# A two-layer graph network with skip LSTMs: the second convolution's positive part moves from ScalarE to VectorE, and the next round's normalisations start two cells later

## The chip, the cores and the metric

The kernel runs on one core of a Trainium2 chip. The metric is the device time of one execution in microseconds. PE is TensorE (the matrix engine), DVE is VectorE, ACT is ScalarE, POOL is GpSimd, SP is the engine that issues the DMAs.

## What is computed

Two blocks, each with a layer norm in front and a residual sum behind. `x` is 128 graphs of 128 nodes with 128 features. The first block works in the eigenbasis of a Laplacian; the change doesn't touch it. The second is the one of interest:

```python
h = jnp.maximum(_layernorm(x, axis=-1), 0.0)
# inside _L1_gnn_ref(h, adj, ...)
h = jax.nn.relu(jnp.einsum('ts,bsh->bth', adj, x @ Wg0 + bg0))
h = jax.nn.relu(jnp.einsum('ts,bsh->bth', adj, h @ Wg1 + bg1))      # the second relu is the one that moves
for p in range(1, MAX_SKIP + 1):                                    # 1 to 4
    nw = Tv // p
    wins = h[:, :nw * p, :].reshape(Bv * nw, p, Hd)
    last = _lstm_last(Wih[p - 1], Whh[p - 1], bih[p - 1], bhh[p - 1], wins)
    idx = jnp.arange(nw) * p + (p - 1)
    h = h.at[:, idx, :].set(last.reshape(Bv, nw, Hd))
```

So for every skip p from 1 to 4 an LSTM of p steps runs over all windows of p nodes, and its last hidden state replaces the window's last node.

## The kernel before

**Stages.** The first 440 us or so compute the eigenvectors (small steps on DVE, ACT, PE and POOL), with parts of the first block behind them until about 748 us. From there to the end the second block runs, on PE, DVE and ACT, with one table load of ACT ahead of it and none inside.

**Rounds and streams.** The second block has 8 rounds (`ROUNDS`). A round holds 4 streams i = 0 to 3 of 4 graphs each. Streams 0 and 1 are one pair (A), 2 and 3 the other (B). Each stream owns two PSUM banks.

**The order.** The list `ORDER` (L155) is the same for PE, ACT and DVE, and each of them walks it in its own program (`second_layer`, L562, L822, L1471), with semaphores between them. An entry (n, i) is step n for stream i. Steps are LIN, ZED (x times the second weight), CONV (times the adjacency), then 11 cells, then TURN. Pair B runs one step behind pair A: after LIN for all four the order is ZED 0, ZED 1, CONV 0, CONV 1, ZED 2, ZED 3, cell0 0, cell0 1, CONV 2, CONV 3, cell1 0, cell1 1, cell0 2, cell0 3, cell2 0 and so on. The cells are `CELLS` (L41): cell0 and cell1 are the two halves of p = 1, cell2 and cell3 the steps j = 0, 1 of p = 2, cell4 to cell6 those of p = 3, cell7 to cell10 those of p = 4. A cell has 256, 256, 168 or 128 columns for p = 1 to 4. Cells with j = 0 have 3 gates and need only the input product; the others have 4 gates and twice the products. The text calls the cell c of stream i "cell c/i".

**One cell.** PE computes the gates (L805, L810 and L815, L818). ACT takes I, G and F out of PSUM with sigmoid or tanh (L552), DVE forms the new state c (L1429 for j = 0; L1432, L1433, L1435 otherwise), ACT takes tanh(c) (`cell_tanh`, L560), DVE multiplies it with the output gate (`hidden`, L1444, L1446). The next cell of the stream on PE waits for that: with j = 0 for all of it, otherwise the input products wait for the tanh and the recurrent products for `hidden`. Both ACT and DVE are one entry late with the second half: `cell_tanh` and `hidden` of a cell are issued inside the next entry of `ORDER`, behind that entry's own first work (`waiting`). ACT issues the output gate behind that.

**The two places that change.** At CONV, ACT waits for `conv_ready[i]` and writes the positive part of 128x512 PSUM elements into `HS[i]` (L574). It reads 512 elements in sequence and writes them with a step of 4 elements, as `HS` holds the four graphs of a node side by side. `H_ready[i]` then lets cell0 of the stream start on PE. `normalize` (L525) forms one graph's normalised input of the next round, 128x128 elements; there are 4 for each stream, issued on ACT behind the output gate of the cells listed in `NORM_AT` (L157), which are 3, 5, 6 and 8. The fourth increments `h1_ready[i]`, for which `mix` (L754) waits at the end of the round on PE. The last round has no normalisations.

**Around them.** DVE at LIN, ZED and TURN handles 128x512 elements each out of PSUM (L1477, L1481, L1455), and copies the next round's `mix` (L1451). In round 0 alone DVE also takes statistics for later normalisations behind some cells (`last_statistics`, L1458: four instructions L1397 behind each stream's cell 3, 5 and 6). SP stores each stream's result (L297) after TURN.

Of the kernel before, what the change touches and what calls it, by code (L numbers as in the profile page):

```python
# [6 lines left out]
ALU = mybir.AluOpType  # L7
ACT = mybir.ActivationFunctionType
# [18 lines left out]
GB = 4  # L27
# [13 lines left out]
CELLS = [(1, 0, 0, N // 2), (1, 0, N // 2, N // 2)] + [(p, j, 0, N // p) for p in range(2, SKIPS + 1) for j in range(p)]  # L41
# [18 lines left out]
def build(nc, t_in, out):  # L60
    with ExitStack() as ctx:
# [3 lines left out]
        def sem(name):  # L65
            return ctx.enter_context(nc.semaphore(name))
# [72 lines left out]
        def per_stream(name):  # L139
# [7 lines left out]
        y_ready, z_ready, z_kept, conv_ready, H_ready = map(per_stream, ("y", "z", "zk", "conv", "H"))  # L147
# [5 lines left out]
        MIX, LIN, ZED, CONV, CELL = range(5)  # L153
        TURN = CELL + len(CELLS)
        ORDER = [(LIN, i) for i in range(STREAMS)]             + [(n, i) for slot in range(ZED, TURN + 1) for pair, n in (((0, 1), slot), ((2, 3), slot - 1))  # L155
               for i in pair if n > LIN] + [(TURN + 1, i) for i in range(STREAMS)] + [(TURN, i) for i in (2, 3)]
        NORM_AT = [c for c, (_, j, _, _) in enumerate(CELLS) if j][:GB]  # L157
        adj_in = sem("adj_in")
        consts = sem("consts")
        v_ = sem("v_")  # L160
# [65 lines left out]
        gI, gF, gG, gO, cS, HS, tS, hS = ([pieces[STREAMS * c + i] for i in range(STREAMS)] for c in range(8))  # L226
# [25 lines left out]
        def batches(v):  # L252
            return v.rearrange("p (b t) -> p b t", b=GB)

        def nodes(v):
            return v.rearrange("p (n b) -> p n b", b=GB)
# [5 lines left out]
        bank = [[banks[2 * i + c % 2][:] for c in range(4)] for i in range(STREAMS)]  # L262
# [160 lines left out]
        def _(act):  # L423
# [98 lines left out]
            def normalize(it, i, b, done):  # L522

                at = bass.ds(batch(it, i, b), 1)
                ins = nc.scalar.activation(hs[i][:, b * D:(b + 1) * D], X[:, at, :].rearrange("p b d -> p (b d)"),  # L525
                                           ACT.Relu, bias=ln[:, 3, at], scale=ln[:, 2, at])
                if b == GB - 1:
                    ins.then_inc(done[i], 1)
# [15 lines left out]
            def gates(it, c, i, qs):  # L544

                p, j, _, nw = CELLS[c]
                T = GB * nw
                for q in qs:
                    if q == GATE_F and j == 0:
                        continue  # L550
                    at = (p - 1) * 4 + q
                    last = nc.scalar.activation(gate_out[q][i][:, 0:T], gate(i, q, T),  # L552
                                                ACT.Tanh if q == GATE_G else ACT.Sigmoid, bias=bias[:, at:at + 1])
                if q == GATE_F:
                    last.then_inc(acts_ready[i], 1)

            def cell_tanh(it, c, i):
                T = GB * CELLS[c][3]
                act.wait_ge(cell_ready[i], it * len(CELLS) + c + 1)
                nc.scalar.activation(tS[i][:, 0:T], cS[i][:, 0:T], ACT.Tanh).then_inc(tanh_ready[i], 1)  # L560

            def second_layer(it, more):  # L562
                act.wait_ge(tables, it + 1)

                nc.scalar.activation(act_scratch[:], ln[:, 2, 0:1], ACT.Sigmoid).then_inc(tables, 1)
                waiting = None
                for n, i in ORDER:
                    c = n - CELL
                    if n == LIN:
                        act.wait_ge(lin_kept[i], it + 1)  # L570
                        nc.scalar.activation(yS[i], linS[i], ACT.Relu).then_inc(y_ready[i], 1)
                    elif n == CONV:
                        act.wait_ge(conv_ready[i], it + 1)
                        nc.scalar.activation(nodes(HS[i]).rearrange("p n b -> p b n"), batches(bank[i][0]),  # L574
                                             ACT.Relu).then_inc(H_ready[i], 1)
                    elif CELL <= n < TURN:
                        act.wait_ge(gates_ready[i], it * len(CELLS) + c + 1)
                        gates(it, c, i, (GATE_I, GATE_G, GATE_F))
                    if waiting:
                        cell_tanh(it, *waiting)  # L580
                        waiting = None
                    if CELL <= n < TURN:
                        gates(it, c, i, (GATE_O,))
                        waiting = (c, i)
                        if more and c in NORM_AT:
                            normalize(it + 1, i, NORM_AT.index(c), h1_ready)

            half = ROUNDS // 2 - 1
            with nc.scalar.Fori(0, half) as it:
                second_layer(it, True)  # L590
            act.wait_ge(ln_done, 3)
            with nc.scalar.Fori(half, ROUNDS - 1) as it:
                second_layer(it, True)
            second_layer(ROUNDS - 1, False)

        B = [b[:, 0:N] for b in banks]
# [248 lines left out]
        def _(dve):  # L845
            t = Tally(v_)
            V = nc.vector
# [308 lines left out]
            for f in range(2, F):  # L1156
                c = f % 2
# [266 lines left out]
            def cell(it, c, i):  # L1424
                p, j, _, nw = CELLS[c]
                T = GB * nw
                dve.wait_ge(acts_ready[i], it * len(CELLS) + c + 1)
                if j == 0:
                    V.tensor_tensor(cS[i][:, 0:T], gI[i][:, 0:T], gG[i][:, 0:T], ALU.mult).then_inc(cell_ready[i], 1)  # L1429
                    return  # L1430
                parts = it * PARTS + sum(2 for _, jj, _, _ in CELLS[:c] if jj)
                V.tensor_tensor(gI[i][:, 0:T], gI[i][:, 0:T], gG[i][:, 0:T], ALU.mult).then_inc(cell_part[i], 1)  # L1432
                V.tensor_tensor(gF[i][:, 0:T], gF[i][:, 0:T], cS[i][:, 0:T], ALU.mult).then_inc(cell_part[i], 1)  # L1433
                dve.wait_ge(cell_part[i], parts + 2)
                V.tensor_tensor(cS[i][:, 0:T], gI[i][:, 0:T], gF[i][:, 0:T], ALU.add).then_inc(cell_ready[i], 1)  # L1435

            def hidden(it, c, i):
                p, j, w0, nw = CELLS[c]
                T = GB * nw

                dve.wait_ge(tanh_ready[i], it * len(CELLS) + c + 1)

                if j < p - 1:
                    V.tensor_tensor(hS[i][:, 0:T], gO[i][:, 0:T], tS[i][:, 0:T], ALU.mult).then_inc(hidden_ready[i], 1)  # L1444
                else:
                    V.tensor_tensor(window(HS[i], p, j, w0, nw), nodes(gO[i][:, 0:T]), nodes(tS[i][:, 0:T]),  # L1446
                                    ALU.mult).then_inc(hidden_ready[i], 1)

            def keep_mix(it, i):
                dve.wait_ge(mix_ready[i], it + 1)  # L1450
                V.tensor_copy(mixS[i], bank[i][0]).then_inc(mix_kept[i], 1)  # L1451

            def residual(it, i):
                dve.wait_ge(turned_ready[i], it + 1)
                V.tensor_tensor(X[:, group(it, i), :], X[:, group(it, i), :], batches(bank[i][1]),  # L1455
                                ALU.add).then_inc(sum_ready[i], 1)
# [14 lines left out]
            def second_layer(it, more, extra=None):  # L1471

                waiting = None
                for n, i in ORDER:
                    if n == LIN:
                        dve.wait_ge(lin_ready[i], it + 1)
                        V.tensor_tensor(batches(linS[i]), batches(bank[i][2]),  # L1477
                                        G0[:].unsqueeze(1).to_broadcast([N, GB, N]), ALU.add).then_inc(lin_kept[i], 1)
                    elif n == ZED:
                        dve.wait_ge(z_ready[i], it + 1)  # L1480
                        V.tensor_tensor(batches(zS[i]), batches(bank[i][3]),  # L1481
                                        bg1B[:].unsqueeze(1).to_broadcast([N, GB, D]), ALU.add).then_inc(z_kept[i], 1)
                    elif CELL <= n < TURN:
                        cell(it, n - CELL, i)
                    elif n == TURN:
                        residual(it, i)
                    elif n > TURN and more:
                        keep_mix(it + 1, i)
                    if waiting:
                        hidden(it, *waiting)  # L1490
                        waiting = None
                    if CELL <= n < TURN:
                        waiting = (n - CELL, i)
                    if extra:
                        extra(n, i)

            for i in range(STREAMS):
                keep_mix(0, i)
            second_layer(0, True, last_statistics)
            with V.Fori(1, ROUNDS - 1) as it:  # L1500
                second_layer(it, True)
# [24 lines left out]
```

## Time and profile before

| | us |
|---|---|
| median of 3 runs | 1515.49 |
| their range | 1513.96 to 1518.14 |
| the profiled execution, own time | 1516.81 |
| its span in the trace | 1515.1 |
| rounds 1 to 6 of the second block, from 848 to 1418 us, each | 94.9 |
| PE, busy share of the span | 79% |
| DVE, ACT, busy share of the span | 73%, 62% |

Times in the rows are microseconds from the start of the span, unless they are marked ns. A line of a timeline gives start, duration, engine and line, what is written and read, and how many like it were merged; in square brackets the idle time of the engine before it, and what ended that. PEld is PE's load of weights. All durations come from one profiled execution. A fp32 matmul shows as two passes, so a product in the program is two rows' worth in the trace.

### The profile page before, as it was taken

How to read it: one execution, taken by the hardware profiler on the slowest of the kernel's cores; microseconds unless marked ns; L12 is line 12 of the kernel's file. 1: busy time of each engine (PE TensorE's matmuls, PEld its weight loads, DVE VectorE, ACT ScalarE, POOL GpSimd, SP SyncE). 2: the span in 40 equal slices, each digit the busy share in tenths (PEclk: the TensorE clock that was granted, in tenths of full speed). 3: DMA queues.
4: the chain of work that ended last, by engine and by line, in shares of the span. 5: the costliest groups of instructions: out<-in, count | busy, mean ns of one | idle time of the engine just before them, and what ended most of it. 6: DMA issues, size and time to landing. Idle time of an engine off the chain costs nothing.

```text
span 1515.1 us, 26850 instructions
## 1 busy us (share of the span) xinstructions
PE 1196.2 (79%) x7121; PEld 1069.9 (71%) x7121; DVE 1107.1 (73%) x5944; ACT 943.2 (62%) x3339; POOL 508.6 (34%) x1426
## 2 busy tenths in 40 slices
PE   5777777777536400179999999999999999999998
PEld 4566666666435300168789899898998989989897
DVE  8999999999999999958747656455564554645545
ACT  4666666666349600012478687786877868778676
POOL 0288888888888888830000200000000000000000
PEclk9999999999869855579999999999999999999999
DMA  9300000000000000003100000000000000000001
GB/s 269 79 1 1 1 1 1 1 1 1 1 1 1 1 0 0 1 28 105 36 1 2 28 0 28 0 0 28 0 28 0 0 28 0 26 2 0 28 1 29
DMA packets 43630, 28.80 MB, mean 19 GB/s; under 512 B 1520, under 2 KB 39440, under 8 KB 43536
## 3 DMA queue, kind: packets, MB, share of 16 engines
q1 hardware_dynamic: 43536, 27.81, 6.7%
q14 instruction: 67, 0.55, 0.1%
q8 instruction: 27, 0.44, 0.1%
HBM read 19.42 MB, written 8.39 MB: 18 GB/s over the span
## 4 chain that ended last, share of the span: by engine, by line
PE 52%; POOL 33%; issue 7%; DVE 6%; ACT 2%; POOLq 0%; ACTq 0%; DVEq 0%
PE bank L815 13%; PE bank L805 10%; POOL leaf L388 9%; PE bank L810 8%; PE bank L818 7%; POOL leaf L386 6%; POOL leaf L403 3%; PE bank L735 2%; PE bank L787 2%; PE bank L779 2%; PE bank L743 2%; PE bank L773 2%; PE bank L750 2%; PE bank L758 2%; ACT BIG L552 1%
## 5 line engine op out<-in xcount | busy, mean ns | idle before, releaser
L815 PE MATMUL bank<-spare,wT 128*128 128x256 f32 (+2 forms) x1408 | 311.3, 321 | 0.0
L552 ACT ACTIVATE PV<-bank,bias 128x256 f32<-128x256 f32 (+2 forms) x704 | 304.0, 435 | 0.0
L552 ACT ACTIVATE BIG<-bank,bias 128x128 f32<-128x128 f32 (+2 forms) x544 | 227.6, 418 | 121.0 <-PE bank L818 101.9
L815 PEld LDWEIGHTS bank<-spare,wT 128*128 128x128 f32 x1408 | 234.8, 191 | 13.2
L805 PE MATMUL bank<-spare,wT 128*128 128x128 f32 (+2 forms) x1088 | 228.1, 320 | 4.1 <-DVE spare L1446 2.7
L1432 DVE TENSOR_TENSOR BIG<-BIG,PV 128x128 f32<-128x128 f32 (+2 forms) x192 | 63.0, 328 | 205.9 <-ACT BIG L552 205.9
L805 PEld LDWEIGHTS bank<-spare,wT 128*128 128x128 f32 x1088 | 168.7, 190 | 22.5 <-DVE spare L1446 9.1
L818 PE MATMUL bank<-spare,wT 128*128 128x128 f32 (+2 forms) x768 | 169.7, 303 | 0.0
L810 PE MATMUL bank<-spare,wT 128*128 128x128 f32 (+2 forms) x768 | 141.6, 307 | 3.8 <-DVE spare L1444 1.4
L618 PE MATMUL bank<-ident 128*128 128x2 f32 x254 | 74.3, 362 | 88.6 <-DVE ident L963 87.5
L388 POOL TENSOR_TENSOR leaf<-leaf 128x1 f32<-128x1 f32 x240 | 136.7, 570 | 20.0
L560 ACT ACTIVATE spare<-spare 128x256 f32<-128x256 f32 (+2 forms) x352 | 134.4, 382 | 6.9 <-DVE spare L1435 6.9
L618 PEld LDWEIGHTS bank<-ident 128*128 128x128 f32 x254 | 63.6, 311 | 99.6 <-DVE ident L963 98.2
L1429 DVE TENSOR_TENSOR spare<-BIG,PV 128x256 f32<-128x256 f32 (+2 forms) x160 | 60.8, 380 | 95.7 <-ACT PV L552 95.6
L818 PEld LDWEIGHTS bank<-spare,wT 128*128 128x128 f32 x768 | 125.2, 191 | 3.3
L810 PEld LDWEIGHTS bank<-spare,wT 128*128 128x128 f32 x768 | 113.8, 191 | 14.2 <-DVE spare L1444 10.9
L386 POOL TENSOR_SCALAR leaf<-leaf 128x1 f32<-128x1 f32 x240 | 93.3, 389 | 23.4
L610 PE MATMUL bank<-ones,sc 128*128 128x1 f32 x2 | 0.6, 348 | 120.5 <-DVE sc L1269 120.5
L442 ACT ACTIVATE sc<-bank 128x1 f32<-128x1 f32 x127 | 21.7, 171 | 116.1 <-PE bank L618 116.0
L623 PE MATMUL bank<-A,UC 128*128 128x127 f32 (+63 forms) x254 | 87.5, 442 | 7.3 <-DVE UC L926 0.8
L1209 DVE SCALAR_TENSOR_TENSOR PV<-RC,m,PV 128x4 f32<-128x4 f32 x508 | 90.6, 220 | 0.0
L610 PEld LDWEIGHTS bank<-ones,sc 128*128 128x128 f32 x2 | 0.5, 313 | 120.6 <-issue 120.6
(405 smaller groups left out, 3000.8 us busy)
## 6 DMA issues: line engine op xcount, KB each, us to landing
spare<-in_x SPq DMA_DIRECT2D x32, 256.0 KB, 3.8
out<-X SPq DMA_DIRECT2D x32, 256.0 KB, 2.4
spare<-in_L_gnn_Wih SPq DMA_DIRECT2D x4, 256.0 KB, 5.2
spare<-in_L_gnn_Whh SPq DMA_DIRECT2D x4, 256.0 KB, 4.6
W<-in_L_gnn_W SPq DMA_DIRECT2D x2, 64.0 KB, 2.7
Wg<-in_L_gnn_Wg SPq DMA_DIRECT2D x2, 64.0 KB, 2.4
adj<-in_adj SPq DMA_DIRECT2D x1, 64.0 KB, 2.0
X<-in_x SPq DMA_DIRECT2D x4, 0.5 KB, 17.0
```

The costliest lines, as they stand in the source:

```text
L386: op(TS(am[:, i + 1:i + 2], rho[:, i:i + 1], ne16[:, i:i + 1], am[:, i + 1:i + 2], ALU.mult, ALU.add))
L388: op(TT(rho[:, i + 1:i + 2], am[:, i + 1:i + 2], neg16[:, 0:1], ALU.pow))
L552: last = nc.scalar.activation(gate_out[q][i][:, 0:T], gate(i, q, T), ACT.Tanh if q == GATE_G else ACT.Sigmoid, bias=bias[:, at:at + 1])
L560: nc.scalar.activation(tS[i][:, 0:T], cS[i][:, 0:T], ACT.Tanh).then_inc(tanh_ready[i], 1)
L618: nc.tensor.matmul(banks[7][:, 0:2], x_wide, ident[:, t:N + 1:N - t], start=True, stop=True).then_inc(s_ready, 1)
L623: nc.tensor.matmul(banks[1][:, live(k)], u_c.to_broadcast([N, N]), A[:, live(k)], start=True, stop=True).then_inc(pb_ready, 1)
L805: last = nc.tensor.matmul(gate(i, q, T), wT[:, 0, p - 1, q * D:(q + 1) * D], xt, start=True, stop=(j == 0))
L810: last = nc.tensor.matmul(gate(i, q, T), wT[:, 1, p - 1, q * D:(q + 1) * D], hS[i][:, 0:T], start=False, stop=True)
L815: last = nc.tensor.matmul(gate(i, q, T), wT[:, 0, p - 1, q * D:(q + 1) * D], xt, start=True, stop=(j == 0))
L818: last = nc.tensor.matmul(gate(i, q, T), wT[:, 1, p - 1, q * D:(q + 1) * D], hS[i][:, 0:T], start=False, stop=True)
L1209: s.did(V.scalar_tensor_tensor(out=nx, in0=RC[:, last + lane:last + lane + live], scalar=M[2][:, row:row + 1], in1=nx, op0=ALU.mult, op1=A ...
L1432: V.tensor_tensor(gI[i][:, 0:T], gI[i][:, 0:T], gG[i][:, 0:T], ALU.mult).then_inc(cell_part[i], 1)
```

## The change

`NORM_AT` takes the first four cells with j > 0 and p > 2: cells 5, 6, 8 and 9 in place of 3, 5, 6 and 8. The positive part at CONV is issued by DVE as a `tensor_scalar` with a maximum against 0, at the same entry of the order and with the same wait, source, destination and semaphore; ACT has nothing of its own to do at CONV any more.

```diff
-        NORM_AT = [c for c, (_, j, _, _) in enumerate(CELLS) if j][:GB]
+        NORM_AT = [c for c, (p, j, _, _) in enumerate(CELLS) if p > 2 and j][:GB]
@@ ACT, second_layer
-                    elif n == CONV:
-                        act.wait_ge(conv_ready[i], it + 1)
-                        nc.scalar.activation(nodes(HS[i]).rearrange("p n b -> p b n"), batches(bank[i][0]),
-                                             ACT.Relu).then_inc(H_ready[i], 1)
@@ DVE, second_layer
+                    elif n == CONV:
+                        dve.wait_ge(conv_ready[i], it + 1)
+                        V.tensor_scalar(nodes(HS[i]).rearrange("p n b -> p b n"), batches(bank[i][0]), 0.0, None,
+                                        ALU.max).then_inc(H_ready[i], 1)
```

## Rows read from the trace of the kernel before

**Rows 1.** The page: busy time of the engines, and the granted clock in slices.

```profile
PE 1196.2 (79%) x7121; PEld 1069.9 (71%) x7121; DVE 1107.1 (73%) x5944; ACT 943.2 (62%) x3339; POOL 508.6 (34%) x1426
...
PEclk9999999999869855579999999999999999999999
```

**Rows 2.** Windows: busy time of each engine in round 3, then granted clock.

```profile
1038.00:1133.00 95.00, 94.06 (x626) 86.31 (x625) 51.05 (x153) 73.61 (x225) 0.00 (x0) 1.00 0.04 11
```

**Rows 3.** Waits in round 3: who waited for whom, total us, times, longest.

```profile
PEld bank L810 <- DVE spare L1444: 1.4, 4, 0.4
PEld bank L805 <- DVE spare L1446: 1.1, 2, 0.7
PEld bank L805 <- ACT spare L560: 0.5, 2, 0.4
```

**Rows 4.** Timeline of PE: first products of cells 1/0, 1/1, 0/2 and 0/3.

```profile
1051.02 0.70 PE L805 MATMUL bank<-spare,wT 128*128 128x256 f32 x2
...
1052.55 0.70 PE L805 MATMUL bank<-spare,wT 128*128 128x256 f32 x2
...
1053.95 0.59 PE L805 MATMUL bank<-spare,wT 128*128 128x256 f32 x2
...
1055.25 0.59 PE L805 MATMUL bank<-spare,wT 128*128 128x256 f32 x2
```

**Rows 5.** Timeline of ACT and DVE at CONV of pair B, round 3.

```profile
1050.55 0.42 DVE L1446 TENSOR_TENSOR spare<-PV,spare 128x256 f32<-128x256 f32 x1
1050.73 1.10 ACT L574 ACTIVATE spare<-bank 128x512 f32<-128x512 f32 x1
...
1051.59 0.45 ACT L560 ACTIVATE spare<-spare 128x256 f32<-128x256 f32 x1
1051.91 1.10 ACT L574 ACTIVATE spare<-bank 128x512 f32<-128x512 f32 x1
1052.07 0.43 DVE L1446 TENSOR_TENSOR spare<-PV,spare 128x256 f32<-128x256 f32 x1 [1.10 <-ACT spare L560]
```

**Rows 6.** Groups by shape: busy us, mean ns, idle before. Last: L533's instructions, ns.

```profile
L574 ACT ACTIVATE spare<-bank 128x512 f32<-128x512 f32 x4 | 4.2, 1111 | 1.5 <-PE bank L787 1.5
...
L1481 DVE TENSOR_TENSOR spare<-bank,bg1B 128x512 f32<-128x512 f32 x4 | 2.8, 692 | 2.7 <-PE bank L779 2.7
...
L533 ACT ACTIVATE PV<-bank,b x32: 687/687/687, 662.8 to 741.1; 128x512 f32<-128x512 f32 x32
```

**Rows 7.** Timeline of DVE at pair A's CONV and pair B's ZED, round 3.

```profile
1043.02 0.69 DVE L1481 TENSOR_TENSOR spare<-bank,bg1B 128x512 f32<-128x512 f32 x1 [0.20 <-PE bank L779]
1044.06 2.04 ACT L574 ACTIVATE spare<-bank 128x512 f32<-128x512 f32 x2 [1.47 <-PE bank L787]
...
1045.85 0.69 DVE L1481 TENSOR_TENSOR spare<-bank,bg1B 128x512 f32<-128x512 f32 x1 [2.14 <-PE bank L779]
```

**Rows 8.** Timeline at cell 3's normalisation: ACT, DVE, then PE's cells 4.

```profile
1070.58 0.50 ACT L525 ACTIVATE ahead<-X,ln 128x128 f32 x1
...
1070.96 0.48 ACT L552 ACTIVATE BIG<-bank,bias 128x256 f32<-128x256 f32 x1
...
1072.18 0.42 DVE L1446 TENSOR_TENSOR spare<-PV,spare 128x256 f32<-128x256 f32 x1
...
1072.65 0.55 PE L805 MATMUL bank<-spare,wT 128*128 128x168 f32 x2
...
1085.13 0.45 PE L805 MATMUL bank<-spare,wT 128*128 128x168 f32 x2
```

**Rows 9.** Timeline of PE: what follows each of the two cells 4 of Rows 8.

```profile
1073.61 1.08 PE L805 MATMUL bank<-spare,wT 128*128 128x256 f32 x4
...
1085.99 0.45 PE L805 MATMUL bank<-spare,wT 128*128 128x168 f32 x2
```

**Rows 10.** Timeline of ACT at cell 9 of pair B, and the PE row behind it.

```profile
1122.72 0.37 ACT L552 ACTIVATE BIG<-bank,bias 128x128 f32<-128x128 f32 x1 [0.45 <-PE bank L818]
...
1123.85 0.71 PE L805 MATMUL bank<-spare,wT 128*128 128x128 f32 x4 [0.18 <-ACT spare L560]
...
1124.49 0.31 ACT L560 ACTIVATE spare<-spare 128x128 f32<-128x128 f32 x1 [0.43 <-DVE spare L1435]
```

**Rows 11.** Timeline of DVE in round 0, behind cell 3 of stream 0.

```profile
785.39 0.87 DVE L1397 BATCH_NORM_STATS2 stats<-X 128x6 f32<-128x128 f32 x4
```

## The prediction

> **What bounds the kernel.** I read the page first, then the windows of the second block, then the waits of one round, then the timeline at each of PE's waits. The page's busy shares [rows 1] average over stages with different limits: over the span DVE is nearly as busy as PE. The change works only in the second block, so its windows count, and there the picture is plain: in round 3 PE is busy 94.06 of 95.00 us, ACT 73.6, DVE 51.1, and the granted clock is 1.00, the 2.4 GHz level [rows 2]. Rounds 1 to 6 read the same to 0.1 us. PE is the bound of this stage. An engine that is relieved gives nothing by itself; only what shortens a wait of PE does.
>
> The waits of the round name those places: PE's weight loads wait 4 times for `hidden` ahead of the recurrent products (1.4 us), twice for `hidden` ahead of a cell with j = 0 (1.1 us), twice for the tanh (0.5 us) [rows 3], 3.0 us in a round and 24 us in eight. That is about all that could be won by anything that leaves the matmuls alone. For each of the places I followed in the timeline what PE waited for, and asked whether ScalarE's positive part (L574) or the normalisation of cell 3 lies in that chain.
>
> **The positive part leaves ACT.** It is issued 32 times at 1.11 us [rows 6], 4 in a round, so ACT loses 4.4 us of its 73.6. ACT is not the bound; what counts is who is queued behind. For pair A (streams 0, 1) ACT issues it while PE is still at pair B's ZED, and nothing on PE waits. For pair B it stands in front of the tanh of cell 0/1: L574 starts at 1050.73, that tanh only 0.86 us later, at 1051.59; `hidden` of cell 0/1 follows at 1052.07 on DVE, idle for 1.10 us before it, and ends at 1052.50 [rows 5]. PE starts cell 1/1 at 1052.55 [rows 4]. This is one of the two j = 0 waits. Its price is read from the cells' lengths on PE: cell 0/2 takes 1055.25 - 1053.95 = 1.30 us undisturbed; cell 1/0 takes 1.53 and cell 1/1 1.40 [rows 4]. The first waited itself for cell 0/0, and its restart shows 0.10 in its own length, which stays, as no L574 is ahead of that. So 1.53 + 1.40 - 1.30 - 1.30 - 0.10 = 0.23 us is the price of the wait of cell 1/1, its restart included. Without L574 the tanh can start at 1050.73, and ends 0.45 later at 1051.18. PE would be free for cell 1/1 at 1051.02 + 1.40 = 1052.42.
>
> **The positive part joins DVE.** Four instructions in a round, on an engine idle for 44 of 95 us [rows 2]. The trace has no `tensor_scalar` of this form, so its length d is bounded. The nearest row for the source and size is L1481, 128x512 out of PSUM on DVE: 0.69 us [rows 6]. It writes in sequence, though, and the new one writes with a step of 4 elements. ACT shows what that step can cost: L574 takes 1.11, L533 with the same source and size but a plain destination 0.687 [rows 6], so 0.42 us more. Upper end 0.69 + 0.42 = 1.11; lower end 0.69. I take the upper half, about 0.95: if the memory's side sets the pace, DVE's slower base hides part of the 0.42.
>
> The Trainium skill says, in "Advanced Engine Details and Errata", section Memory Cachelines, that successive accesses run at full rate only inside the same 16-byte line of SBUF, and that a new line for each access costs. Here every one of the 512 writes of four bytes lands in a new line. The L574 and L533 rows agree with it [rows 6]; the page gives no price for DVE, and by a step that costs nothing the sum would be the one for d = 0.69.
>
> What is queued behind it on DVE: for pair A, the ZED of pair B. Conv 0 is out at 1044.06, where L574 starts; two positive parts of 0.95 to 1.11 end at about 1046.0 to 1046.2, and L1481 of stream 2, which starts at 1045.85 after an idle of 2.14 [rows 7], is 0.1 to 0.4 us late. PE uses its result only at pair B's CONV, behind two whole cells; hidden. If that cover were gone it would cost that 0.1 to 0.4. For pair B, the positive part of stream 2 stands in front of `hidden` of cell 0/1, exactly as L574 stood in front of the tanh. DVE is free for it at about 1050.55 + 0.35 = 1050.90 (the 0.42 us instructions start 0.35 apart; conv 2 is out by then, as L574 started at 1050.73 without idle). So `hidden` of cell 0/1 ends at 1050.90 + d + 0.42 at the latest: 1052.01 for 0.69, 1052.27 for 0.95, 1052.43 for 1.11. PE wants it at 1052.42. With d = 0.95 the wait is gone, 0.23 us; with 1.11 it begins to return. The next positive part, of stream 3, ends before 1053.4 and its cell 0/3 runs on PE from 1055.25 - 0.23.
>
> **The normalisation of cell 3 goes to cell 9.** Four per stream as before, so ACT's sum is unchanged. At cell 3 of stream 1, L525 starts at 1070.58 and the gates of cell 2/2 at 1070.96: it holds ACT 0.38 us [rows 8]. On these gates hangs the state of cell 2/2, which DVE forms ahead of `hidden` of cell 3/1, at 1072.18 to 1072.60, and PE starts cell 4/1 at 1072.65 [rows 8]. Cell 4/1 takes 0.96 us, an undisturbed cell 4 takes 0.86 [rows 8, 9]: a restart of 0.10 us. PE was ready at about the same instant, so the 0.38 us on ACT buys these 0.10 and no more. The large part of the wait in front, at cell 4/0, comes straight from PE through gates, state and `hidden`, with ACT idle ahead of it; no normalisation is in it. In round 0 the statistics L1397 hold DVE for 0.87 us there [rows 11], and nothing is gained; the last round has no normalisations. So 6 x 0.10.
>
> What it costs at cell 9: behind pair B's output gate ACT was idle 0.45 us until the gates of cell 9/3 came from PE at 1122.72, and 0.43 us before the tanh at 1124.49 [rows 10]. A normalisation holds ACT 0.38, so both fit, by 0.07 and 0.05 us. They must: PE's cell 10/2 waits for the tanh behind those gates already, with 0.18 us idle [rows 10]. If the cover failed, each 0.1 us of overrun would cost 0.7 us in seven rounds. For pair A the idle times are as long and PE has two cells of pair B as cover. `h1_ready` comes one cell later, and PE asks for it only behind all four cells 10. SP's stores and POOL have no part in either move.
>
> **The sum.** 8 x 0.23 + 6 x 0.10 = 2.4 us. Against the profiled execution's own 1516.81 that is 1514.4; this execution lies 1.32 above the median of the runs, so the median becomes 1515.49 - 2.4 = 1513.1, or 0.16% less. About 0.3% (4.5 us) is what a measurement of this kernel can tell from no change, so the forecast is "no difference".
>
> **Rivals.**
> (a) The wait comes back in another coat: if d is 1.2 to 1.35, `hidden` of cell 0/1 ends at about the old 1052.50 or a little behind. The 1.84 us are lost or turned, only the 0.6 stay: 1514.9 to 1516. For it: the step's cost, unseen on DVE. Against: even ACT's extra of 0.42 gives 1.11.
> (b) Slower: the strided write on DVE costs several times as much. It pays from d = 1.35 upwards; at d = 2.0 `hidden` of cell 0/1 ends at 1050.90 + 2.0 + 0.42 = 1053.3, 0.9 us after PE wants it, plus 0.1 restart, in place of 0.23: 0.77 a round, 8 x 0.77 - 0.6 = 5.6 us more, 1521.1. Against it: neither bound reaches there.
> (c) More is gained than the chains show: if the wait at cell 4/0 (longest 0.7 us [rows 3]) shrinks too once ACT is lighter, 8 x 0.55 = 4.4 more, 1508.7. Against it: ACT idles ahead of the gates it stems from.
> (d) Normalisations at cell 9 overrun their slot by 0.1 to 0.2 us in seven rounds, 0.7 to 1.4: 1514.
>
> **How the numbers follow.** Forecast 0.58, (a) 0.15, (b) 0.08, (c) 0.08, (d) 0.11. The range takes the forecast with the ends of d, (a), (d), and the 1 to 2 us by which medians of so few runs differ: 1510.3 to 1516.9. Faster by over 0.3% (under 1510.9) is (c) with a little of the forecast's edge, 0.10; slower (over 1520.0) is (b), 0.07; within, 0.83.
>
> **What would show it.** A DVE row of L574's shape with d between 0.69 and 1.11; cells 1/0 and 1/1 on PE at 1.40 and 1.30 in place of 1.53 and 1.40; cell 4/1 at 0.86; the loops' rounds 0.33 us shorter than 94.9; PE's wait at cell 10/2 unchanged at 0.18. The prediction is wrong if d is above 1.3, if a new wait of PE stands at a cell 1 or at a cell 10, or if a round changes by more than 0.6 us.

## The result and the profile after

| | before | after |
|---|---|---|
| median, 15 runs each | 1516.02 us | 1512.95 us |
| ratio | | 0.9979, 95% interval 0.9971 to 0.9987 |
| profiled execution, own time | 1516.81 us | 1513.86 us |
| rounds 2 to 6 of the second block, each | 94.87 us | 94.45 us |

The change saves 0.21%, 3.1 us of medians. The forecast was 2.4 us, called "no difference", since about 0.3% was taken as the least that a measurement of this kernel can tell. With 15 runs each the interval is clear of 1, so as little as 0.2% can be told; it leaves room for a saving between 2.0 and 4.4 us, and the rounds say more exactly what the change did.

The page after has the engines' shares moved as the edit says: DVE up by 27 us, ACT down by 29, PE down by 3.4 [rows 1].

```profile
PE 1192.8 (79%) x7121; PEld 1069.7 (71%) x7121; DVE 1134.5 (75%) x5976; ACT 913.9 (60%) x3307; POOL 509.2 (34%) x1426
...
PEclk9999999999869855579999999999999999999999
```

The chain that ended last, after, gives the rounds: start in the span, duration, and what it was. The first product of LIN marks each round (L769 after is L773 before; lines behind L571 moved up by 4 on ACT's side).

```profile
942.32 3.44 PE bank L769 x8
...
1036.77 3.44 PE bank L769 x8
...
1131.23 3.44 PE bank L769 x8
...
1225.68 3.44 PE bank L769 x8
```

1131.23 - 1036.77 = 94.46 (94.45 as the mean of rounds 2 to 6); before it was 94.87. In this round of after, the waits of PE's weight loads for other engines (who waited for whom, us in total, times, longest) are:

```profile
PEld bank L806 <- DVE spare L1440: 1.4, 4, 0.4
PEld bank L801 <- DVE spare L1442: 0.7, 1, 0.7
PEld bank L801 <- ACT spare L560: 0.5, 2, 0.4
```

Against [rows 3] one line has changed: ahead of cells with j = 0 there is one wait where there were two. The timeline of PE shows the cells of [rows 4] and [rows 8, 9] after:

```profile
1050.04 0.70 PE L801 MATMUL bank<-spare,wT 128*128 128x256 f32 x2
1051.44 0.59 PE L801 MATMUL bank<-spare,wT 128*128 128x256 f32 x2
1052.73 0.59 PE L801 MATMUL bank<-spare,wT 128*128 128x256 f32 x2
...
1071.41 0.45 PE L801 MATMUL bank<-spare,wT 128*128 128x168 f32 x2
1072.27 1.03 PE L801 MATMUL bank<-spare,wT 128*128 128x256 f32 x4
```

Cell 1/0 now takes 1051.44 - 1050.04 = 1.40 us and cell 1/1 1.29, against 1.53 and 1.40: 0.24 us. Cell 4/1 takes 0.86 against 0.96, and the first four rows of cell 3/2 behind it 1.03 against 1.08. Both kernels issue the same matmuls in the same order, so the start of each row can be compared, counted from the start of the round; the text calls that "product for product". In round 3 the two kernels differ in five steps only: 0.132 and 0.104 us at cell 1/1, 0.023 and 0.104 at cell 4/1, 0.054 at cell 3/2. That is 0.417 of the 0.42.

What took the positive part's place, on ACT and DVE after (as [rows 5] before):

```profile
1049.57 0.42 DVE L1442 TENSOR_TENSOR spare<-PV,spare 128x256 f32<-128x256 f32 x1
1049.74 0.42 ACT L560 ACTIVATE spare<-spare 128x256 f32<-128x256 f32 x1
1049.90 1.07 DVE L1481 TENSOR_SCALAR spare<-bank 128x512 f32<-128x512 f32 x1
...
1050.81 0.41 DVE L1442 TENSOR_TENSOR spare<-PV,spare 128x256 f32<-128x256 f32 x1
```

The tanh of cell 0/1 follows its neighbour at once, the positive part takes 1.07 us on DVE, and `hidden` behind it starts 0.91 us after it, not 1.07. It ends at 1051.22, and PE starts cell 1/1 at 1051.44 without a wait.

In round 0 only the first of the two gains shows, 0.23 us at cell 1/1, and in the last one too (93.34 against 93.62 from its first product to PE's end), as forecast. Round 1 is not like rounds 2 to 6, though the prediction read rounds 1 to 6 as the same: from LIN to LIN it took 95.20 us before and 94.57 after. Of these 0.63 us 0.20 lie at the start of ZED; round 0, from LIN to LIN, became only 0.04 shorter, so rounds 0 and 1 together gain 0.67, which is 0.24 + 0.42 within 0.01.

### The profile page after: what moved, and what is told of

Its sections match the earlier page's. It is cut to its first block, busy times and chain, and to the rows that moved or that the text cites. A ratio compares the mean times of both kernels' runs of the same rounds, so it can differ in the third digit from the quotient of the medians.

```text
span 1512.1 us, 26850 instructions
## 1 busy us (share of the span) xinstructions
PE 1192.8 (79%) x7121; PEld 1069.7 (71%) x7121; DVE 1134.5 (75%) x5976; ACT 913.9 (60%) x3307; POOL 509.2 (34%) x1426
## 4 chain that ended last, share of the span: by engine, by line
PE 52%; POOL 34%; issue 7%; DVE 6%; ACT 2%; POOLq 0%; ACTq 0%; DVEq 0%
PE bank L811 13%; PE bank L801 9%; POOL leaf L388 9%; PE bank L806 8%; PE bank L814 7%; POOL leaf L386 6%; POOL leaf L403 3%; PE bank L731 2%; PE bank L783 2%; PE bank L739 2%; PE bank L775 2%; PE bank L769 2%; PE bank L746 2%; PE bank L754 2%; ACT BIG L552 1%
## 5 line engine op out<-in xcount | busy, mean ns | idle before, releaser
L560 ACT ACTIVATE spare<-spare 128x256 f32<-128x256 f32 (+2 forms) x352 | 133.1, 378 | 4.2 <-DVE spare L1431 3.9
```

## The experiments

Rounds are read as above, from the starts of LIN in rounds 2 to 6. They repeat within 0.02 us in a trace (0.04 in e9), and the products that an edit doesn't touch keep their pace from one kernel's trace to the next, so one profiled execution of each kernel is used where the rounds are the measure; e3 to e6 ran only once. The times of whole kernels carry more: the second block began anywhere from 748.6 us (e2) to 753.7 us (e6) in the profiled executions, and no edit touches the work ahead of it.

### One edit alone

e1 moves the positive part and leaves the normalisations:

```diff
-        NORM_AT = [c for c, (p, j, _, _) in enumerate(CELLS) if p > 2 and j][:GB]
+        NORM_AT = [c for c, (_, j, _, _) in enumerate(CELLS) if j][:GB]
```

> The positive part goes to VectorE, the normalisations stay at cells 3, 5, 6 and 8. My theory (the two edits remove two separate waits of PE): the wait at cell 1/1 is gone as in the changed kernel, the late start of cell 4/1 stays; rounds 2 to 6 take 94.87 - 0.24 = 94.63 us, the whole kernel 1.8 to 2.0 us less than before. Rival (one edit does all, the other is idle): 94.45 us, 3 us less. A second rival (the gain needs both, since the ACT time freed is what counts): 94.87, nothing gained.

e2 is the kernel before with the new `NORM_AT` alone.

> The normalisations go to cells 5, 6, 8 and 9, the positive part stays on ScalarE. My theory: the wait of 0.24 us at cell 1/1 stays, cells 4/1 and 3/2 start 0.18 us earlier in all rounds but the first and the last; rounds 2 to 6 take 94.87 - 0.18 = 94.69 us, the whole kernel 1.1 us less than before, and cell 10/2's wait is unchanged. Rivals: nothing gained (94.87), as PE would have been later anyway; or all of the 0.42 us (94.45).

Measured: e1 94.65 us a round, e2 94.68. The kernels: 1516.86 and 1516.47 us where the kernel before took 1518.34 on the same chip, ratios 0.9991 (0.9982 to 1.0000) and 0.9990 (0.9981 to 0.9999). These intervals are too wide to tell the two edits apart; the rounds can. PE's cells in e1, then in e2:

```profile
1051.38 0.70 PE L801 MATMUL bank<-spare,wT 128*128 128x256 f32 x2
1052.78 0.59 PE L801 MATMUL bank<-spare,wT 128*128 128x256 f32 x2
...
1072.78 0.55 PE L801 MATMUL bank<-spare,wT 128*128 128x168 f32 x2
1073.74 1.08 PE L801 MATMUL bank<-spare,wT 128*128 128x256 f32 x4
```

```profile
1047.85 0.70 PE L805 MATMUL bank<-spare,wT 128*128 128x256 f32 x2
1049.37 0.70 PE L805 MATMUL bank<-spare,wT 128*128 128x256 f32 x2
...
1069.45 0.45 PE L805 MATMUL bank<-spare,wT 128*128 128x168 f32 x2
1070.31 1.03 PE L805 MATMUL bank<-spare,wT 128*128 128x256 f32 x4
```

In e1 cell 1/0 takes 1.40 (gone) and cell 4/1 0.96 (still late); in e2 it is 1.52 and 0.86. The gains, 0.22 and 0.19 us, add up to 0.41, where both together give 0.42. Two separate waits, as the theory had it; both rivals fall.

### The positive part of pair B twice: how much room is in front of `hidden`

e3 is the changed kernel with this ahead of the positive part, for streams 2 and 3 (e4, below, for streams 0 and 1):

```diff
+                        if i in (2, 3):
+                            V.tensor_scalar(nodes(RC[:, i % 2 * GW:(i % 2 + 1) * GW]).rearrange("p n b -> p b n"),
+                                            batches(bank[i][0]), 0.0, None, ALU.max)
                         V.tensor_scalar(nodes(HS[i]).rearrange("p n b -> p b n"), batches(bank[i][0]), 0.0, None,
```

> The changed kernel with the positive part of streams 2 and 3 computed twice on VectorE (the first time into a scratch tile with the same step). My theory (the positive part stands ahead of hidden of cell 0/1, which has 0.2 us to spare): the second one holds VectorE 0.91 us more, hidden of cell 0/1 ends about 0.7 us after PE wants it, PE's wait returns with 0.7 to 0.9 us; rounds 2 to 6 take 95.2 to 95.4 us, the kernel 6 to 7.5 us more than the changed one. Rival (VectorE idles 40 us of a round, so its own time is free): 94.45 us, no difference.

Measured: 95.30 us a round; the second block took 6.8 us more than in the changed kernel, as expected. The single time of the whole kernel, 1522.15 us beside 1515.75 of the kernel before, can't be set against the changed one, which didn't run beside it. The two DVE rows and the PE row that waits for them, in e3:

```profile
1053.94 1.06 DVE L1482 TENSOR_SCALAR RC<-bank 128x512 f32<-128x512 f32 x1
...
1054.84 1.07 DVE L1484 TENSOR_SCALAR spare<-bank 128x512 f32<-128x512 f32 x1
...
1055.75 0.41 DVE L1442 TENSOR_TENSOR spare<-PV,spare 128x256 f32<-128x256 f32 x1
...
1056.22 0.70 PE L801 MATMUL bank<-spare,wT 128*128 128x256 f32 x2 [0.58 <-DVE spare L1442]
```

The extra instruction holds DVE 0.90 us. Product for product, cell 1/1 starts 0.745 us later than in the changed kernel and its second row loses 0.104 more. So `hidden` had 0.90 - 0.745 = 0.16 us of room. Though VectorE is idle for 40 us of the round, all that went beyond this room was paid for in full at this place. The rival that its time is free falls.

### The positive part of pair A twice: the cover

e4 puts the same extra instruction ahead of the positive part of streams 0 and 1.

> The same for streams 0 and 1. My theory (cover by two cells of PE behind pair B's ZED): the two extra ones make the ZED instructions of pair B up to 2 us late, and PE needs them 2.6 us after their end; rounds 2 to 6 stay at 94.45 us within 0.1. Rival: they make PE wait at CONV of pair B or at cell 0/0, 0.3 us a round or more.

Measured: 94.69 us, 0.24 more than the changed kernel. A miss. I had looked at who is queued behind on DVE (ZED of pair B) and not at the extra instructions' own result. DVE and PE in e4:

```profile
1046.35 1.10 DVE L1484 TENSOR_SCALAR spare<-bank 128x512 f32<-128x512 f32 x1
...
1047.28 1.29 DVE L1477 TENSOR_TENSOR spare<-bank,bg1B 128x512 f32<-128x512 f32 x2
1047.51 0.70 PE L801 MATMUL bank<-spare,wT 128*128 128x256 f32 x2
```

The last of the four instructions, shown above, writes `HS` of stream 1, out at 1047.45, and cell 0/1 on PE starts at 1047.51: it waits for `H_ready[1]`. Product for product, all of the loss is there, 0.144 and 0.105 us. ZED of pair B, late by 1.6 to 1.9 us (two run at 1047.28), costs nothing; that part held. The rival named cell 0/0 or CONV of pair B and 0.3 us or more: it was right that this place has little cover, and near in place and price.

### A plain destination: what the step of 4 elements costs

```diff
-                        V.tensor_scalar(nodes(HS[i]).rearrange("p n b -> p b n"), batches(bank[i][0]), 0.0, None,
+                        V.tensor_scalar(batches(HS[i]), batches(bank[i][0]), 0.0, None,
```

e5 writes in sequence. It computes something else, as the cells read another arrangement, with the same amount of work.

> The changed kernel with the positive part written in sequence instead of with a step of 4 elements; the cells then read the nodes and graphs in another arrangement, so what is computed differs, with the same amount of work. My theory (the length of 1.08 us comes from the step alone): each takes 0.68 to 0.70 us, and as the wait at cell 1/1 is gone at 1.08 already, rounds 2 to 6 stay at 94.45 us. Rival (a tensor_scalar out of PSUM is slow whatever its destination): about 1.08 still.

Measured: 94.47 us a round, and in the groups by shape (busy us, mean ns, idle before) in e5, then in the changed kernel:

```profile
L1481 DVE TENSOR_SCALAR spare<-bank 128x512 f32<-128x512 f32 x4 | 2.8, 688 | 0.6 <-PE bank L783 0.6
```

```profile
L1481 DVE TENSOR_SCALAR spare<-bank 128x512 f32<-128x512 f32 x4 | 4.1, 1077 | 0.4 <-PE bank L783 0.4
```

The step costs 0.39 us of 512 elements on DVE, nearly the 0.42 of ACT [rows 6], and a plain one is as long as the `tensor_tensor` of ZED, L1481 before (0.692). The rival, that the instruction is slow whatever its destination, falls. The shorter one buys nothing in the round, since the wait is gone at 1.08 already.

### Two normalisations at cell 9: the slot

e6 is the changed kernel with normalisations behind cells 5, 6, 9 and 9 (`NORM_AT = [5, 6, 9, 9]`, and a loop that issues both at cell 9).

> The changed kernel with two normalisations at cell 9 and none at cell 8. My theory (one holds ScalarE 0.38 us in an idle time of 0.45, so two overrun it by about 0.3): the gates of cell 9/3 and the tanh behind them start 0.3 us late, PE's wait at cell 10/2 grows by as much; rounds 2 to 6 take 94.7 to 94.9 us. Rival (there is more slack than that row shows): 94.45 us.

Measured: 94.67 us, 0.21 more than the changed kernel, all of it at cell 10/2. ACT in e6:

```profile
1123.27 0.38 ACT L552 ACTIVATE PV<-bank,bias 128x128 f32<-128x128 f32 x1
1123.52 0.88 ACT L525 ACTIVATE ahead<-X,ln 128x128 f32 x2
1124.29 0.37 ACT L552 ACTIVATE BIG<-bank,bias 128x128 f32<-128x128 f32 x1
```

Place and sign as expected, size a third smaller, just below the expected 94.7 to 94.9. Two normalisations hold ACT 1124.29 - 1123.52 = 0.77 us, 0.385 each. How long the slot is shows in the changed kernel, with one normalisation in it:

```profile
1120.74 0.50 ACT L525 ACTIVATE ahead<-X,ln 128x128 f32 x1
1121.31 0.37 ACT L552 ACTIVATE BIG<-bank,bias 128x128 f32<-128x128 f32 x1
```

Counted from start to start it is 1121.31 - 1120.74 = 0.57 us, where the prediction read 0.45 from an idle time, which begins only at the end of the instruction before. One normalisation therefore leaves 0.19 us, not 0.07, and two overrun by 0.20, which is what PE lost (0.204). In the changed kernel the wait at cell 10/2 is as it was [rows 10]:

```profile
1122.45 0.71 PE L801 MATMUL bank<-spare,wT 128*128 128x128 f32 x4 [0.18 <-ACT spare L560]
```

### The waits that were left: a version that beats both

The prediction read one of the large waits, at cell 4/0, as coming from PE through gates, state and `hidden`, with ACT idle ahead of the gates. That suggests a cause, for it and for four more like it: `cell_tanh` and `hidden` of the stream before are issued behind the next entry's gates, though they could run while ACT and DVE wait for these. e7 turns that round at five places:

```diff
+        EARLY = ((3, 0), (5, 0), (5, 2), (8, 0), (9, 2))
@@ ACT, second_layer, first in the loop over ORDER
+                    if waiting in EARLY:
+                        cell_tanh(it, *waiting)
+                        waiting = None
@@ DVE, second_layer, first in the loop over ORDER
+                    if waiting in EARLY:
+                        hidden(it, *waiting)
+                        waiting = None
```

> The changed kernel, and behind five cells (3/0, 5/0, 5/2, 8/0 and 9/2) the tanh of the state on ScalarE and the hidden product on VectorE are issued ahead of the next entry's own work, not behind it. My theory: the waits that are left on PE (cell 4/0 0.56 us, cell 6/0 0.28, cell 6/2 0.65, cell 9/0 0.50, cell 10/2 0.86) are latency made by that order of issue, since ScalarE idles before the next gates; most of the 2.85 us a round goes: rounds 2 to 6 take 91.6 to 92.3 us, the kernel 1490 to 1496 us. Rival (the chain from PE through gates, state and tanh is itself that long, or the neighbour's gates slip by as much): rounds stay at 94.2 to 94.6, with the waits moved to the neighbouring stream's cell.

Measured: 91.97 us a round, inside the expected range; the kernel, at the edge of its range, 1496.03 us where the kernel before took 1518.34, ratio 0.9852 (0.9837 to 0.9867). ACT now takes the tanh of cell 3/0 in its idle time, ahead of the gates of cell 3/1:

```profile
1061.46 0.42 ACT L561 ACTIVATE spare<-spare 128x256 f32<-128x256 f32 x1 [0.62 <-DVE spare L1435]
...
1062.42 0.47 ACT L553 ACTIVATE BIG<-bank,bias 128x256 f32<-128x256 f32 x1 [0.55 <-PE bank L818]
```

The window of a round in e7 (length, then busy us of PE, its weight loads, DVE, ACT and POOL, then granted clock), against 94.06 of 95.00 in [rows 2]:

```profile
1031.40:1123.40 92.00, 91.99 (x627) 85.99 (x626) 54.99 (x157) 70.11 (x221) 0.00 (x0) 1.00 0.04 12
```

Of the waits for other engines one is listed:

```profile
PEld bank L805 <- DVE spare L1446: 0.3, 1, 0.3
```

Product for product, the steps at the five places are gone, 2.86 us: 0.56 at cell 4/0, 0.28 at 6/0, 0.65 at 6/2, 0.51 at 9/0 and 0.86 at 10/2. Of these 0.36 came back at cells 4/1 and 3/2, the neighbour's, as the rival had it in kind: 2.49 net. That is more than PE's idle time in the changed kernel's round, 94.50 - 93.57 = 0.93 us. A row of PE is longer when the next one starts late (0.410 us against 0.306 at the late cell 4/1 before), so part of a wait counts as busy: at cell 4/0 the trace shows 0.29 us of idle time, and the wait cost 0.56.

e9 puts the same five early issues on the kernel before the change.

> The early issue behind the same five cells, put on the kernel before the change (positive part on ScalarE, normalisations at cells 3, 5, 6, 8). My theory (the five waits and the two that the change removes are separate): rounds 2 to 6 take 94.87 - 2.49 = 92.38 us, 0.42 more than with the change, and the kernel 3 us more than that version. Rival (with the tanh issued early ScalarE needs the time that the change frees, or the normalisation at cell 3 no longer matters): between 92.0 and 92.2, or above 92.6 us.

Measured: 92.28 us a round, 0.31 more than e7, between the theory's 92.38 and the 92.0 to 92.2 of its rival; the kernel 1495.96 us beside 1516.69 of the kernel before, ratio 0.9869 (0.9852 to 0.9885). The times of e7 and e9 come from two chips and can't be set against each other; the rounds can. Product for product, the 0.23 us at cell 1/1 is as in e1. At cells 4/1 and 3/2 the normalisation costs 0.07 (0.102 less 0.032), and not 0.18, as PE waits at cell 4/1 in both versions. So the waits of the change and those of the early issue are separate but for that place.

## Why the prediction was right

Point by point, as it stands:

- **PE bounds, only its waits count.** Right. ACT lost 29 us and DVE gained 27, and the kernel moved by 3; e3 and e4 show the other side, DVE work at a place with no room costs at once. The 3.0 us of waits in a round are no strict limit, though: the change and e7 together took out steps of 0.42 + 2.86 = 3.28 us, of which 0.36 came back.
- **Positive part off ACT, 8 x 0.23.** Right: 0.236 in a round of the traces, 0.23 in e1.
- **Its length on DVE, 0.69 to 1.11, taken as 0.95.** Inside, at the upper end: 1.08. The reason given for 0.95, that DVE's slower base would hide part of the step, was wrong: e5 shows the step costing 0.39 on top of 0.69. The rule of the Trainium skill, "Advanced Engine Details and Errata", section Memory Cachelines, agrees with e5 in kind: the writes that each land in a new line were slower, by 0.39 us for 512. No run separates the line from the step as the cause.
- **When the wait would return.** The prediction put that at d = 1.11, which would have left 1.08 about 0.02 us of room. It counted the full length as the time to the next instruction; DVE starts the next 0.91 us after a 1.07 us one. From e3 the room was 0.16, so the wait returns at about 1.08 + 0.16 = 1.24. Rival (a) was put at 1.2 to 1.35, and rival (b), slower, from 1.35; an estimate from e3's room puts both some 0.1 higher. That the gain came whole doesn't confirm the prediction's working of the room, as the real room was larger.
- **Normalisation off cell 3, 6 x 0.10.** Right in place, too small in size: 0.19, by e2. The prediction took only cell 4/1's own stretch, 0.104. PE also waited 0.023 for it, and the second row of cell 3/2 behind it ran 0.054 late, visible in [rows 9] as 1.08 for four rows where 1.03 is usual. The row stood there and was not read. That is 6 x 0.09 = 0.5 us, most of the difference between 2.4 and 3.1. That the gain is missing in round 0 is so (e2: no step at cell 4/1 there); that the statistics are the reason was not tested.
- **Cell 9 takes it.** Right that it costs nothing; the margin was 0.19, not 0.07 (e6), from taking an idle time for a slot. The price of an overrun was right: 0.20 us cost 0.21 a round in e6. Rival (d) didn't happen.
- **Pair A's cover.** Right in the result, incomplete in the reason: the next one waiting was cell 0/1 for `H_ready[1]`, not ZED (e4).
- **Rival (c), the wait at cell 4/0 shrinking with a lighter ACT.** Didn't happen: 0.29 us idle on PE before and after. e7 shows it needs the order of issue, not a lighter engine.
- **The median.** The forecast 1513.1 and the measured 1512.95 lie 0.15 us apart, and that is partly luck: the saving was 0.7 us larger than forecast, and the median before, over 15 runs, 0.5 us higher than the 1515.49 that the forecast started from.

The sum with the measured terms: 7 x 0.236 + 0.27 for the last round, where the wait was 0.04 longer, + 6 x 0.19 = 3.1 us. The second block is 3.05 us shorter in the two profiles; the medians' 3.1 agree, within a much wider interval.

## What to carry to other kernels

Where one engine is busy 99% of a stage, list its waits in one round and price each from the lengths of its own neighbouring pieces: the total (here 3.0 us of 95, of which 2.9 were won in the end) is about what reshuffling can give, and each edit gives what stands in one of these chains, however many microseconds it moves between the others. Then ask of each wait that is left whether the engine in front of it was idle while work it could have done stood behind its next wait: here five such places were worth six times the change, 2.49 us a round against 0.42. Measure slots and room from start to start, since an idle time begins only when the last instruction ends.

## What the runs showed of the hardware

- A 128x512 write with a step of 4 fp32 elements costs 0.39 us more than a plain one on VectorE (1.077 against 0.688) and 0.42 more on ScalarE (1.11 against 0.687).
- VectorE starts the next instruction before the end of the last: 0.91 us after the start of a 1.07 us one.
- In this kernel a wait of TensorE cost more than its length: at every place where a change took a wait away or brought one in, the row behind the first one moved by a further 0.10 us (0.101 to 0.105, for 128, 168 and 256 columns), also where the first was held only 0.02 us (cell 4/1). At cell 3/2 before, the tanh (L560, from 1073.05, 0.46 long) ended at 1073.51, 0.10 us ahead of the row at 1073.61 that reads it, and the next row still came 0.05 late.
